# A decoder layer: the slots' queries are folded into the key weights in the mixer's last chunk but one instead of in the tables stage, and the cross output weights are fetched behind that

## What is computed

```python
x = _layernorm(x + _L0_attn_ref(...))    # mixer: x @ W_in.T, 4-tap convolution, chunked state scan, @ W_out.T
x = _layernorm(x + _L0_xattn_ref(...))   # cross attention to 77 context rows, 16 heads of 32
x = _layernorm(x + _L0_ffn_ref(...))     # 16 slots attend to the tokens, 16 experts on the slots, tokens attend to the slots
```

```python
q = jnp.broadcast_to(slot_query, (Bx, NS, D))
qh = (q @ d_Wq + d_bq).reshape(Bq, Lq, H, dh)
kh = (x @ d_Wk + d_bk).reshape(Bq, -1, H, dh)
scores = jnp.einsum('bqhd,bkhd->bhqk', qh, kh) / jnp.sqrt(dh)
```

## Time and profile before

| | before |
|---|---|
| median of 3 runs | 1627.88 us (1625.83 to 1629.79) |
| profiled execution, its time | 1620.04 us |
| profiled execution, span from first to last instruction | 1618.4 us |
| TensorE's granted clock over the span | 0.941 of full |
| PE busy | 1388.2 us, 86% |
| DVE busy | 806.8 us, 50% |

### The profile page before, as it was taken

One profiled execution on the slowest core, in us unless ns is written; L12 is line 12 of the kernel. 1 busy time (PEld: TensorE's weight loads), 2 busy tenths in 40 slices (PEclk: granted clock), 3 DMA queues, 4 the chain that ended last, 5 costly groups with the idle time before them and its releaser, 6 DMA issues. The chain is left out here.

```text
span 1618.4 us, 26476 instructions
## 1 busy us (share of the span) xinstructions
PE 1388.2 (86%) x9892; PEld 869.9 (54%) x9892; DVE 806.8 (50%) x2195; ACT 449.9 (28%) x938; POOL 234.4 (14%) x209
## 2 busy tenths in 40 slices
PE   6899999999989899989999975866666666668996
PEld 3777777776667677767777753211111111116663
DVE  0656667767766577766776753000000000003997
ACT  2434444342234334444444331000000000001333
POOL 1111111100121121211212201000000000001221
PEclk9899999999999899999999987999889888989999
DMA  9342223222112411341111117999999999981563
GB/s 352 124 130 92 78 67 92 92 79 65 60 53 72 183 52 56 132 164 53 45 52 45 45 40 269 388 425 427 423 426 427 424 427 425 425 346 53 193 210 130
DMA packets 76038, 309.22 MB, mean 191 GB/s; under 512 B 9803, under 2 KB 14923, under 8 KB 58552
## 3 DMA queue, kind: packets, MB, share of 16 engines
q1 hardware_dynamic: 74680, 307.91, 49.6%
q0 software_dynamic: 1024, 0.27, 0.1%
q10 hardware_dynamic: 256, 0.00, 0.0%
HBM read 274.33 MB, written 33.82 MB: 190 GB/s over the span
## 5 line engine op out<-in xcount | busy, mean ns | idle before, releaser
L1440 PE MATMUL exp_bank<-all_ring,exp_hm 128*32 128x512 f32 x976 | 151.2, 734 | 102.8 <-DMA all_ring<-in_e_W 55.0
L1476 DVE TENSOR_TENSOR exp_gu<-exp_up,exp_gate 128x512 f32<-128x512 f32 x16 | 11.1, 692 | 400.3 <-ACT exp_gate L1485 400.3
L152 PE MATMUL mix_bank<-all_ring,mxw_win 128*128 128x256 f32 x672 | 156.5, 386 | 2.1 <-POOL all_ring L1330 2.1
L1440 PEld LDWEIGHTS exp_bank<-all_ring,exp_hm 128*32 128x32 f32 x976 | 31.0, 122 | 208.3 <-DMA all_ring<-in_e_Wg 76.6
L152 PEld LDWEIGHTS mix_bank<-all_ring,mxw_win 128*128 128x128 f32 x672 | 126.4, 192 | 28.5 <-issue 9.0
L1104 POOL TENSOR_TENSOR mxw_win<-mxw_win 128x1232 f32<-128x1232 f32 x32 | 72.2, 2257 | 422.5 <-DVE mxw_win L1069 422.5
L1462 PE MATMUL exp_bank<-all_ring,exp_guT 128*32 128x512 f32 x512 | 111.9, 647 | 15.5 <-DVE exp_guT L1479 12.5
L903 PE MATMUL mix_bank<-mxw_win,att_q_w 128*128 128x128 f32 x1024 | 119.8, 275 | 0.0
L903 PEld LDWEIGHTS mix_bank<-mxw_win,att_q_w 128*128 128x128 f32 x1024 | 116.9, 192 | 0.7 <-issue 0.5
L942 PE MATMUL mix_bank<-att_o_w,mxw_win 128*128 128x512 f32 x256 | 115.3, 593 | 0.0
L222 DVE SCALAR_TENSOR_TENSOR all_ring<-all_ring,mxw_taps 128x256 f32<-128x256 f32 x192 | 84.4, 482 | 53.0 <-ACT all_ring L171 50.4
(11 more groups left out here) (273 smaller groups left out, 2234.7 us busy)
## 6 DMA issues: line engine op xcount, KB each, us to landing
all_ring<-in_e_W SPq DMA_DIRECT2D x62, 2048.0 KB, 26.1
all_ring<-in_e_Wg SPq DMA_DIRECT2D x31, 2048.0 KB, 27.1
all_ring<-in_xT SPq DMA_DIRECT2D x8, 1024.0 KB, 7.8
all_ring<-scratch_rates SPq DMA_DIRECT2D x64, 128.0 KB, 4.2
all_z<-in_x SPq DMA_DIRECT2D x16, 512.0 KB, 4.4
mxw_win<-scratch_x SPq DMA_DIRECT2D x32, 256.0 KB, 2.8
scratch_x<-crs_x SPq DMA_DIRECT2D x32, 256.0 KB, 2.0
scratch_x2T<-crs_x2T SPq DMA_DIRECT2D x32, 256.0 KB, 2.0
```

What stands on the lines that cost most here:

```text
L152: last = nc.tensor.matmul(bank[:, i * BT:(i + 1) * BT], hold["win"][:, k, m * P:(m + 1) * P], hold["xT"][b % 2][:, k, :], start=(k == 0), ...
L1440: last = nc.tensor.matmul(bank[w][q * ROWS:(q + 1) * ROWS, :], hm[u][:, k, :], weights[:, at:at + FQ], start=(k == 0), stop=False)
```

## The change

The fold leaves the tables stage. `sqbd` and the semaphore of `d_WkT` move to tiles that live on into the mixer. PE does the 16 matmuls in chunk 14, after `score` and before `add_to_state`, into the two projection banks (`fold_slots`). ACT copies the two banks into `m1` with two instructions instead of four (`take_slots`). Since `d_WkT` now lies in `o_w` until chunk 14, SP loads the cross output weights there and no longer in chunk 1. It waits for `m1_ready` first, and the load of `ob` stands behind that. PE waits for `m1_done` before it turns the first tile, and for `o_in` before it first uses `o_w`.

```diff
 # tables_stage, tensor
-                pe.wait_ge(s["kT_in"], 16)
                 pe.wait_ge(s["sq_ready"], 1)
-                pe.wait_ge(s["norm_steps"], 1)
-                for k in range(KC):
-                    for g in range(GROUPS):
-                        last = nc.tensor.matmul(M1[k][:, g * HG * SLOTS:(g + 1) * HG * SLOTS], wkT[:, g, k * P:(k + 1) * P],
-                                                sqbd[:, g, :, :], start=True, stop=True)
-                    last.then_inc(s["m1_ready"], 1)
                 pe.wait_ge(s["rates_out"], 1)
 # tables_stage, scalar
-                for k in range(KC):
-                    act.wait_ge(s["m1_ready"], k + 1)
-                    nc.scalar.activation(hold["m1"][:, k, :], M1[k][:, 0:SROWS], ACT.Copy).then_inc(s["m1_done"], 1)
 # mixer_parts
+    def fold_slots(pe):
+        pe.wait_ge(hold["kT_in"], 16)
+        pe.wait_ge(s["proj_out"], LAST_PAIR + 1)
+        for k in range(KC):
+            for g in range(GROUPS):
+                last = nc.tensor.matmul(PROJ[k // 2][:, (k % 2) * SROWS + g * HG * SLOTS:(k % 2) * SROWS + (g + 1) * HG * SLOTS],
+                                        hold["o_w"][:, g, k * P:(k + 1) * P], hold["sqbd"][:, g, :, :], start=True, stop=True)
+        last.then_inc(s["m1_ready"], 1)
+
+    def take_slots(act):
+        act.wait_ge(s["m1_ready"], 1)
+        for i in range(2):
+            nc.scalar.activation(hold["m1"][:, 2 * i:2 * i + 2, :].rearrange("p k r -> p (k r)"), PROJ[i][:], ACT.Copy).then_inc(s["m1_done"], 1)
 # cross_rows, turn_x1 at t == 0
+            pe.wait_ge(mix["m1_done"], 2)
 # cross_rows, project_out at t == 0
+            pe.wait_ge(hold["o_in"], 16)
 # cross_rows, sync
                 if c == 1:
-                    for dst, src in ((hold["q_w"], io["q_w"]), (hold["o_w"], io["o_w"])):
-                        sp.dma_start(dst[:], src.rearrange("(k p) n -> p k n", p=P)).then_inc(hold["cross_in"], 16)
+                    sp.dma_start(hold["q_w"][:], io["q_w"].rearrange("(k p) n -> p k n", p=P)).then_inc(hold["cross_in"], 16)
 ...
                     load(sp, 1, 1)
+                    sp.wait_ge(mix["m1_ready"], 1)
+                    sp.dma_start(hold["o_w"][:], io["o_w"].rearrange("(k p) n -> p k n", p=P)).then_inc(hold["o_in"], 16)
                     sp.dma_start(ob[:], broadcast(io["o_b"].rearrange("(o n) -> o n", o=1), [P, D])).then_inc(s["ob_in"], 16)
 # cross_rows, tensor
                 first["project"](pe, q)
+                if c == END - 1:
+                    first["fold_slots"](pe)
                 first["add_to_state"](pe, c)
 # cross_rows, scalar
                 first["take"](act, q)
+                if c == END - 1:
+                    first["take_slots"](act)
```

More of the change, by code:

```diff
@@ L129 @@
               "b_turned", "btok_done", "x_turned", "xs_done", "scores_done", "scores_masked", "state_done",
-              "state_added", "y_done", "yT_done", "out_done", "res_done", "ln_step", "stats_done", "x1_done")
+              "state_added", "y_done", "yT_done", "out_done", "res_done", "m1_ready", "m1_done", "ln_step", "stats_done", "x1_done")
 def cb_pairs(q):
@@ L260, in tables_stage @@
         slotT = st.sb("slotT", [P, KC, SLOTS])
-        sqbd = st.sb("sqbd", [P, GROUPS, HG, SLOTS])
+        sqbd = hold["sqbd"]
         bank = st.banks()
         PROJ, RATES = bank[6:8], bank[5]
-        M1, KBIAS = (bank[0], bank[1], bank[3], bank[4]), bank[5]
-        s = st.sems("consts", "zeros", "small", "wdt_in", "ctx_in", "kw_in", "vw_in", "qw_in", "kT_in", "vb_in", "slot_in", "taps_in", "blk_used",
+        KBIAS = bank[5]
+        s = st.sems("consts", "zeros", "small", "wdt_in", "ctx_in", "kw_in", "vw_in", "qw_in", "vb_in", "slot_in", "taps_in", "blk_used",
                     "dt_ready", "softplus", "dt_steps", "a_ready", "a_turned", "atok_ready", "cum_ready", "exp_ready",
                     "sums1", "sums2", "carry_steps", "norm_steps", "tables_ready", "tables_done", "rates_turned", "rates_out", "rates_stored", "k_ready", "v_ready", "vtok_ready",
-                    "q_ready", "sq_ready", "m1_ready", "kbias_ready", "kbd_done", "m1_done")
+                    "q_ready", "sq_ready", "kbias_ready", "kbd_done")
         blk_in = [st.sem(f"blk_in{i}") for i in range(3)]
@@ L320, in _ @@
                 weights_in(wq, io["d_Wq"], s["qw_in"])
-                weights_in(wkT, io["d_WkT"], s["kT_in"])
+                weights_in(wkT, io["d_WkT"], hold["kT_in"])
                 mixer_tokens(1)
@@ L800, in mixer_parts @@
                 add_to_state=add_to_state, weigh_steps=weigh_steps, project_out=project_out, take_b=take_b, take=take, normalise=normalise,
-                weigh_x=weigh_x, mask_scores=mask_scores, advance_state=advance_state, rate_outputs=rate_outputs, residual=residual, norm=norm,
+                weigh_x=weigh_x, mask_scores=mask_scores, advance_state=advance_state, rate_outputs=rate_outputs, fold_slots=fold_slots, take_slots=take_slots, residual=residual, norm=norm,
                 state=state, x1_stored=x1_stored, last_pair=LAST_PAIR)
@@ L1196, in _ @@
             first["turn"](pe, END)
-            pe.wait_ge(hold["cross_in"], 3 * 16)
+            pe.wait_ge(hold["cross_in"], 2 * 16)
             turn_x1(pe, 0, 0, 0)
@@ L1295, in _ @@
             first["mask_scores"](dve, END)
-            dve.wait_ge(hold["cross_in"], 3 * 16)
+            dve.wait_ge(hold["cross_in"], 2 * 16)
             take_queries(dve, 0)
@@ L1970, in decoder_layer @@
             hold["m1"] = att.sb("m1", [P, KC, SROWS])
+            hold["sqbd"] = att.sb("sqbd", [P, GROUPS, HG, SLOTS])
             hold["q_w"] = att.sb("q_w", [P, KC, D])
@@ L1974, in decoder_layer @@
             hold["qbias"] = att.sb("qbias", [P, GROUPS])
-            hold["cross_in"] = att.sem("cross_in")
+            hold["cross_in"], hold["o_in"], hold["kT_in"] = att.sem("cross_in"), att.sem("o_in"), att.sem("kT_in")
             with Stage(nc, "mxw") as mxw:
```

## The result

The changed kernel has a median of 1631.22 us over 22 runs, the kernel before 1626.77 over 22 runs taken beside them. The ratio is 1.0027, with a 95% interval of 1.0014 to 1.0040. That is 4.4 us slower, between 2.3 and 6.5. (One run of the kernel before took 2603 us; it stands among the 22 but is not in the ratio, and without it the median is 1626.65.) The forecast for the change was +2.9 us.

What follows compares the result with a forecast made beforehand. The prediction took DVE to bound the tables stage's end and PE and DVE, handing work to each other, to bound chunk 14. It summed 0 + 2.93 + 0 = +2.9 us, to 1630.8 us, range 1626.8 to 1636.

Steps and rivals of the forecast that it cites:

- Nothing gained in the tables stage: At the tables stage's end, DVE drains last at 76.5 us with or without the fold, so removing it gains 0.
- The longer gap costs nothing: Before the mixer, PE idles from about 69 to 78 us; the clock is already at 0.50, so cost 0.
- The fold at the full clock, 3.55 us: In chunk 14, the moved fold takes 3.5 to 3.7 us at clock 1.00, taken as 3.55.
- The rival in which the clock is low during the fold: In chunk 14, the fold takes 6.99 us: 1634.3, or 1637.5 if the clock stays low behind it; chance 0.25.
- Of it 0.62 us is covered, +2.93 in all: In chunk 14, the fold covers only PE's 0.62 us wait for DVE's masked scores, so all behind shifts 2.93 us.
- The transfers are hidden: The later loads of `o_w` and `ob` cost 0, with at least 17 us of room before tile 2's turn.
- The rival of tile 1: In the cross attention, the shift removes tile 1's low clock from 470.5 to 477 us, returning 3.25: 1627.6; chance 0.13.
- The total: For the whole kernel, +2.9 us on the median of 1627.88, giving 1630.8 us, 0.18% slower.
- Theory B: Account set against the prediction in the experiments: about 1.5 us more lost elsewhere, above all by PE's longer idle time.

Runs made afterwards that it cites:

- e1: The changed kernel with the fold left out everywhere and m1 set to zero: ratio 1.0008 to the kernel before, 1.3 us slower.
- e6: The kernel before with each matmul of the fold in the tables stage done twice: ratio 1.0078, 12.7 us slower.
- e7: The kernel before with two of DVE's last three convolutions in the tables stage given to ACT and POOL, the fold unmoved: ratio 1.0001.
- e8: The changed kernel with the edits of e7 and e5 together: ratio 1.0003 to the kernel before, 0.5 us slower.
- e2: The changed kernel with the fold done in the tables stage as well, that result unused: ratio 1.0037 to the kernel before, 6.0 us slower.
- e0: The changed kernel again without an edit, timed beside the experiments: ratio 1.0034 to the kernel before, 5.5 us slower.
- e5: The changed kernel with the fold one place earlier in PE's list, ahead of chunk 14's scores: ratio 1.0012 to the kernel before, 2.0 us slower.
- e9: The changed kernel with each matmul of the fold in chunk 14 done twice: ratio 1.0066 to the kernel before, 10.7 us slower.
- e3: The kernel before with only the cross output weights' load moved from chunk 1 to chunk 14, the fold unmoved: ratio 1.0001.
- e10: The changed kernel with the mixer's first projection done in PE's gap at the tables stage's end: ratio 1.0023 to the kernel before, 3.7 us slower.

## Why the prediction was right, by its steps

**Nothing gained in the tables stage.** Shown. The mixer began 14.3 us after L426 with the fold gone (14.4 before), DVE last. e1 has no fold at all and is not faster. e6 and e7 show both sides of the cover: double PE's part and DVE waits 5.86 us, shorten DVE's and it waits 4.97. One sentence of the prediction goes too far: without the convolutions the fold would not have cost all of its 6.99 us there. SP drained at 72.5 us in the kernel before, 4.0 ahead of DVE, and in e8, with both lists short, SP was last and 3.1 us were gained.

**The longer gap costs nothing.** Not contradicted, and no more than that: e2 fills the gap and is not faster than e0, but its interval leaves room for about 1.5 us. In the traces the first chunk takes 17.2 to 18.6 us with and without the gap.

**The fold at the full clock, 3.55 us.** Measured 3.63, at a granted clock of 1.00, a little over half of the 6.99 us that it took in the tables stage at 0.50. The rival in which the clock is low during the fold did not occur in the profiled executions. That the clock can be low at this place, e1 and e6 show.

**Of it 0.62 us is covered, +2.93 in all.** Measured +2.87. e5 shows that the cover is the wait next to which the work stands, and e9 that nothing else there gives way.

**The transfers are hidden.** Shown in the traces of e3 and of the changed kernel, where PE waits for no transfer in the first tiles; POOL started at 415.3, ahead of the 418.1 that was the worst case.

**The rival of tile 1** (the low clock goes away there) did not come true in the profiled execution, which has two such stretches; e0's execution has none of their cost over the kernel before. So it varies between executions of one kernel, and nothing shows that the change moves it.

**The total.** Forecast +2.9, measured +4.4 (2.3 to 6.5). The forecast of the change lies inside. That the 1630.8 us stood only 0.4 from the median is in part luck: the three runs that it was added to had a median 1.1 above that of the 22, and the change came out 1.5 above the forecast.

The size is not fully explained. Several variants with the fold moved or doubled lost more in the median than their place shows: e0 5.5 against 2.9, e2 6.0 against 3.5 (with its 0.6 in the tables stage), e6 12.7 against 5.8, e9 10.7 against 6.4, and e10 lost 3.7 where its places gained 0.7. In all but e0 the place's figure is outside the interval. Theory B named a cause, PE's idle gap, and e2 leans against that.

The mean granted clock of each timed run says something about it. Over the 87 runs of before beside the experiments, 0.001 less of it goes with 0.82 us more: the 13 runs at 0.939 or higher took 1619.9 to 1623.0 us, the 7 at 0.931 or lower 1626.5 to 1631.3. The runs of e0 have 0.9337 on average, those of before 0.9357. By that slope this is an estimated 1.6 us of the 4.5 by which the means differ, and the 2.9 that are left are chunk 14's. In e6 the clock is 0.9275 against 0.9353, an estimated 6.4 us, of which 1.5 only say that the added matmuls themselves ran at half clock; of the 13.0 by which the means differ, 8.1 are left against 5.8 in its place. In e2 (0.9353) and e9 (0.9345, before 0.9347) the clock is nearly that of before. So about 2 us beyond their places stay without a cause in e2, e6 and e9, and 3 in e10. Whether a shift of the program makes low-clock stretches more frequent, or e0's clock was lower by chance, no run decides.

## What to carry to other kernels

Before work is moved off an engine at a stage's end, read which engine drains last: here 7 us of TensorE lay under 8 us of VectorE, and taking them away moved nothing. In chunk 14, where PE and DVE hand the work to each other, the moved work cost its duration less the one wait it stood next to, so its place in the list is worth reading wait by wait: ahead of the 2.09 us wait it cost 1.35 us of the chunk, behind it 2.9. The gap that the move opened returned something only when work from behind the barrier was put in it: 3.5 us in its place, and less in the whole kernel. And where single executions differ by 10 us, one profile for each kernel shows what a place costs, not what the total is.

## What the runs showed of the hardware

The same 16 float32 matmuls of 64 columns against 128 x 128 weights took 6.99 us in the tables stage at a granted clock of 0.50 and 3.63 in the mixer at 1.00, that is at 1.2 and at 2.4 GHz. In the mixer PE came from matmuls of 128 and 512 columns; in the tables stage it came from matmuls of 16 columns, and the clock stayed at 0.50 although PE was in these matmuls for 6.98 of 7.00 us. The Trainium skill ("TensorE: Matmul & The Clock Gate", "Part 1: The HAM clock gate") says that the clock is low by default and that activity lifts it. The mixer's matmuls, at a granted clock of 1.00, agree with it. The tables stage does not bear it out: the earlier trace rows have 0.50 over 7.0 us of PE's work, and in e6 the doubled fold filled 13.0 us at 0.53. The clock is therefore read from its own column of the windows, not from the busy share.

One kernel's executions differ by 10 to 12 us (1619.20 to 1631.33 in the 35 runs of the kernel before beside e0), in a program whose instructions and waits are the same, and the slower ones have the lower granted clock. In the profiles of the table above the differences lie in the cross attention, where the changed kernel's first profile has two low-clock stretches in the first tiles and the kernel before one, and in the experts and combine stages.
